# Scans of a state-space layer: B and C spread over the channels by DMA through DRAM, products with B on GpSimd, sums of neighbours by identity products on TensorE

## What is computed

```python
def _ssm_layer(x, A_log, Dp, W_dbc, W_dt, b_dt):
    A = -jnp.exp(A_log)
    dbc = jnp.einsum('ble,ce->blc', x, W_dbc)
    delta, Bm, Cm = jnp.split(dbc, [DT_RANK, DT_RANK + N_STATE], axis=-1)
    delta = jax.nn.softplus(jnp.einsum('blr,er->ble', delta, W_dt) + b_dt)
    dA = jnp.exp(delta[..., None] * A)
    dBx = (delta * x)[..., None] * Bm[:, :, None, :]
    _, hs = jax.lax.associative_scan(combine, (dA, dBx), axis=1)   # h = dA * h_before + dBx
    y = jnp.einsum('blen,bln->ble', hs, Cm)
    return y + Dp * x
for i in range(3):
    x = _ssm_layer(x, ...)
    if i < 2:                                # neighbours in time are averaged: 750, 375, 187 steps
        x = x[:, :l // 2 * 2].reshape(b, l // 2, 2, d).mean(axis=2)
```

## Time and profile before

| | us |
|---|---|
| median of 3 runs | 861.51 (857.21 to 864.0) |
| the profiled execution, its own time | 856.02 |
| its span, first to last instruction | 854.2 |
| first scan starts | 44.5 |
| last unit's last scan starts | 367.4 |
| attention's first matmul | 371.9 |

### The profile page before, as it was taken

How to read it: one execution, slowest core, us unless ns; L and a number is a source line. 1 busy time by engine, 2 the same in 40 slices (tenths; PEclk the granted TensorE clock), 3 DMA queues, 4 the chain that set the end, 5 groups by cost and what they waited for, 6 DMA issues and landing times.

```text
span 854.2 us, 10724 instructions
## 1 busy us (share of the span) xinstructions
PE 749.1 (88%) x3396; PEld 379.1 (44%) x3396; DVE 567.9 (66%) x861; ACT 364.0 (43%) x638; POOL 482.0 (56%) x508
## 2 busy tenths in 40 slices
PE   4689888889888887855998889879999999999997
PEld 2345454545545453423776667733233232323232
DVE  3299899999999996846458888656444444444443
ACT  2345455554545554312454555343333433333332
POOL 2379788888888887423565555343333443334331
PEclk9699999999999998967999999999999999999999
DMA  8200000000000000040000000091933444324400
GB/s 308 66 1 1 1 1 2 0 2 1 2 0 1 1 1 0 1 99 1 1 1 3 5 3 3 10 189 43 204 75 78 91 97 96 84 64 95 102 1 18
DMA packets 19078, 37.40 MB, mean 44 GB/s; under 512 B 2255, under 2 KB 17607, under 8 KB 18375
## 3 DMA queue, kind: packets, MB, share of 16 engines
q1 hardware_dynamic: 18711, 36.01, 18.1%
q10 hardware_dynamic: 304, 0.63, 0.2%
HBM read 34.72 MB, written 1.92 MB: 43 GB/s over the span
## 4 chain that ended last, share of the span: by engine, by line
PE 64%; DVE 16%; ACT 8%; issue 6%; POOL 1%; DVEq 0%; ACTq 0%; POOLq 0%
PE pair L706 21%; PE pair L378 12%; PE pair L714 10%; PE pair L379 5%; PE pair L605 4%; DVE tmp L1089 4%; PE pair L588 3%; PE pair L637 2%; ACT work L757 2%; ACT work L758 2%; DVE pair L1062 1%; PE pair L435 1%; PE pair L467 1%; DVE tmp L1097 1%; ACT pair L764 1%
## 5 line engine op out<-in xcount | busy, mean ns | idle before, releaser
L1337 DVE TENSOR_TENSOR hidden<-pair,tmp 128x502 f32<-128x502 f32 (+1 forms) x192 | 121.7, 675 | 144.3 <-PE pair L706 135.2
L1496 POOL TENSOR_TENSOR hidden<-xs,big 128x502 f32<-128x502 f32 (+1 forms) x96 | 111.4, 1162 | 184.2 <-PE pair L706 165.1
L945 ACT ACTIVATE tmp<-pair 128x502 f32<-128x502 f32 (+1 forms) x192 | 102.5, 587 | 174.6 <-PE pair L706 174.6
L1520 POOL TENSOR_TENSOR big<-big 94x512 f32<-94x512 f32 (+3 forms) x120 | 89.6, 780 | 79.6 <-DVE big L1244 71.0
L706 PE MATMUL pair<-xs,w 64*128 64x502 f32 (+1 forms) x384 | 107.6, 638 | 2.4 <-ACT tmp L945 2.4
L714 PE MATMUL pair<-hidden,w 128*64 128x502 f32 (+1 forms) x384 | 101.9, 609 | 2.5 <-DVE hidden L1337 2.5
L706 PE MATMUL pair<-hidden,w 64*128 64x502 f32 (+1 forms) x384 | 98.0, 586 | 0.4
L1089 DVE TENSOR_TENSOR_SCAN tmp<-tmp,pair 128x750 f32<-128x750 f32 (+1 forms) x56 | 95.5, 1706 | 0.1
L775 ACT ACTIVATE tmp<-big,picked 128x749 f32<-128x749 f32 (+2 forms) x56 | 51.1, 913 | 86.6 <-issue 49.5
L378 PE MATMUL pair<-big,work 128*128 128x512 f32 x128 | 67.5, 609 | 11.9 <-ACT work L758 3.6
L1358 POOL TENSOR_TENSOR big<-big,work 128x750 f32<-128x750 f32 (+1 forms) x28 | 45.5, 1624 | 48.4 <-ACT big L762 48.4
(11 more groups left out here) (187 smaller groups left out, 1262.5 us busy)
## 6 DMA issues: line engine op xcount, KB each, us to landing
big<-dispatched SPq DMA_DIRECT2D x40, 502.0 KB, 6.6
big<-in_x SPq DMA_DIRECT2D x3, 1500.0 KB, 11.2
big<-dispatched SPq DMA_DIRECT2D x8, 498.0 KB, 5.7
w<-in_w SPq DMA_DIRECT2D x5, 512.0 KB, 6.9
big<-in_x SPq DMA_DIRECT2D x4, 375.0 KB, 3.5
out<-resid SPq DMA_DIRECT2D x8, 187.0 KB, 7.3
packed<-in_packed ACTq DMA_DIRECT2D x1, 424.5 KB, 4.5
dispatched<-hidden SPq DMA_DIRECT2D x8, 47.0 KB, 1.5
```

What stands on the lines that cost most here:

```text
L945: act.activation(sT[i % 2][:, 0:w], bank[i % 2][:, 0:w], ACT.Silu).then_inc(silu_a, 1)
L1337: v.tensor_tensor(hidT[i % 4][:, 0:w], bank[2 + i % 2][:, 0:w], sT[i % 2][:, 0:w], ALU.mult)\
L1496: pool.tensor_tensor(xw[e % 4][:, 0:hi - lo], xs[:, lo:hi], wx[:, e, 0:hi - lo], ALU.mult)\
L1520: ins = eng.tensor_tensor(dst[:, :, at:at + H * m].rearrange("p u (h d) -> p u h d", d=m), t[:, :, :, 0:m], t[:, :, :, k:D], ALU.mult)
```

## The change

Per unit, by the diff:

- `weighted_b` and `weighted_c` (four wide products) go. In their place `rows(n)` computes only the eight rows that are wanted (two halves of the batch, B and C, two states) with a 32-column matrix `rowsel`; ACT copies them to SBUF (`rows_out`), SP writes them to a DRAM tensor `rowsd` by two DMAs, waits until they have landed, and reads them back by four DMAs, each of which repeats the rows over 64 partitions: into `Bt` (two) and `Ct` (two), both in SBUF and double-buffered by unit. SP does this in order of units, with its waits in the same queue.
- `load(n, j)`, B times u, moves from DVE to POOL and works in place in `Bt`. `recur` now reads dA and `Bt`, `read` reads h and `Ct`, `corrected` reads W and E: both operands in SBUF.
- `pool_output` and `add` go from POOL. In their place PE adds the three terms and their even and odd halves by products with the identity into one PSUM bank (`sums`: six matmuls of 375 or 374 columns), and ACT copies the sum to the next layer's x (`sums_out`, once per unit, twice in layer 2). h and the skip term get a second buffer each.
- `read(n, 1)` moves to the start of DVE's next period. E gets a second buffer, delta and u a ring of seven units. The steps that choose the states use other PSUM banks and are placed a little differently.
- At the start SP loads x for phases 2 and 3 after the rows of unit 0 and unit 1, and the 15 DMAs of `later` (weights of attention and experts) after those of unit 2.

```diff
-        delta = [big[:, 12000 + 3000 * i:15000 + 3000 * i] for i in range(2)]
-        u = [big[:, 18000 + 3000 * i:21000 + 3000 * i] for i in range(2)]
...
-        dA, hT = two(0, 750), two(1500, 750)
-        PT, y0T, E, R, pT = (work[:, 750 * i:750 * i + 750] for i in range(5))
-        sel = [[[work[:, 3375 + 128 * (4 * i + 2 * j + k):3503 + 128 * (4 * i + 2 * j + k)] for k in range(2)]
-                for j in range(STATIC)] for i in range(2)]
+        dA = two(0, 750)
+        hT = [two(1500, 750), two(5250, 750, work)]
+        PT, R, W = (work[:, 750 * i:750 * i + 750] for i in range(3))
+        E, y0T = two(2250, 750, work), two(3750, 750, work)
+        pT = W
+        rowsel = [sb(f"rowsel{i}", [128, 32]) for i in range(2)]
+        rowsT = [sb(f"rows{i}", [64, 375]) for i in range(2)]
...
+            def spread_rows(n):
+                _, l, w, _ = unit(n)
+                i, half = n % 2, w // 2
+                sp.wait_ge(rw_a, n + 1)
+                after(sp, b_d[i], 32 * (n // 2))
+                after(sp, c_d[i], 32 * (n // 2))
+                for c in range(2):
+                    sp.dma_start(rowsd[i, :, :, :, half * c:half * c + half].rearrange("b k j t -> (b k j) t"),
+                                 rowsT[i][32 * c:32 * c + 8, 0:half]).then_inc(rw_d, 16)
+                sp.wait_ge(rw_d, 32 * (n + 1))
+                for k, (dst, sems) in enumerate(((Bt, b_d), (Ct, c_d))):
+                    after(sp, hc_v if k else sc_v, STATIC * (n - 1))
+                    for b in range(2):
+                        sp.dma_start(dst[i][64 * b:64 * b + 64, :, 0:w],
+                                     rowsd[i, b:b + 1, k, :, 0:w].to_broadcast([64, STATIC, w])).then_inc(sems[i], 16)
             load(0)
             sp.wait_ge(params_in, PARAMS)
...
-            sp.wait_ge(xa_g, STATIC * UNITS)
+            for n in range(UNITS):
+                spread_rows(n)
+                if n == 0:
+                    load(5)
+                elif n == 1:
+                    load(6)
+                elif n == 2:
+                    sp.wait_ge(zeroed, 1)
+                    for dst, src in later:
+                        sp.dma_start(dst, src).then_inc(later_in, 16)
+            sp.wait_ge(xa_a, TAKEN[-1])
...
+            def rows(n):
                 p, _, w, x = unit(n)
                 pe.wait_ge(sel_a, p + 1)
-                if j == 0:
-                    pe.wait_ge(relu_a, min(n + 2, UNITS))
+                after(pe, rw_a, n)
+                for c in range(2):
+                    mm = pe.matmul(bank[4][32 * c:32 * c + 32, 0:w // 2], rowsel[p % 2][:, :],
+                                   x[:, w // 2 * c:w // 2 * c + w // 2], start=True, stop=True)
+                mm.then_inc(rw_p, 1)
...
+            def sums(n, part):
+                _, l, _, _ = unit(n)
+                terms = [y0T[n % 2]] + hT[n % 2]
+                if l < 2:
+                    if part == 0:
+                        after(pe, xa_a, TAKEN[n] - 1)
+                        pe.wait_ge(y_v, n + 1)
+                    pe.wait_ge(hc_v, STATIC * n + part + 1)
+                    for i in ((0, 1), (2,))[part]:
+                        for k, t in enumerate(halves(terms[i], l)):
+                            mm = pe.matmul(parts(bank[5], l), ident, t, start=(i == 0 and k == 0), stop=(i == 2 and k == 1))
+                    if part == 1:
+                        mm.then_inc(pl_p, 1)
                 else:
-                    after(pe, sc_v, STATIC * n)
-                    pe.wait_ge(cor_v, min(n + 2, UNITS))
-                    if n == UB[p] and p:
-                        pe.wait_ge(more_v, MV[p])
-                wide(pairs[j], sel[p % 2][j][0], x, w).then_inc(b_p, 1)
...
+                ends = last_of(n) is not None
+                old = n - 1 if n > 0 and last_of(n - 1) is None else None
+                if n > 0 and last_of(n - 1) is not None:
+                    pe.wait_ge(more_v, MV[last_of(n - 1) + 1])
+                if n > 0 and chain(n - 1)[1] in (0, 1):
+                    pe.wait_ge(dec_v, chain(n - 1)[0] * DECV + (3, 6)[chain(n - 1)[1]])
                 if n + 2 < UNITS:
                     z(n + 2)
-                if here:
-                    weighted_c(n, 1)
+                    if not ahead(n + 2):
+                        rows(n + 2)
+                if old is not None:
+                    sums(old, 0)
                 if q == 0:
...
+                if 0 <= n + 1 < UNITS:
+                    summed(n + 1)
...
+                if old is not None:
+                    sums(old, 1)
...
                 if n + 2 < UNITS:
-                    if q == 0:
-                        pe.wait_ge(dec_v, p * DECV + 2)
                     mixed(n + 2)
-                if last_of(n) is not None:
+                    if ahead(n + 2):
+                        rows(n + 2)
+                if q == 0:
+                    extremes_row(p, 0)
+                    extremes_spread(p, 0)
+                elif q == 1:
+                    ranks_and_quadratic(p, 0)
+                if ends:
+                    sums(n, 0)
+                    sums(n, 1)
                     more_slots(last_of(n))
...
-                act.wait_ge(exp_a, n + 1)
-                act.activation(d, e, ACT.Ln, bias=1.0).then_inc(log_a, 1)
-                after(act, sc_v, STATIC * (n - 1))
-                act.activation(pairs[1][:, 0:w], e, ACT.Identity, bias=1.0).then_inc(one_a, 1)
+                z, d, e = pairs[0][:, 0:w], of(delta, n), E[n % 2][:, 0:w]
+                if part == 0:
+                    act.wait_ge(z_p, n + 1)
+                    after(act, dl_g, n - 1)
+                    act.activation(e, z, ACT.Abs, bias=bdt[:, l:l + 1]).then_inc(abs_a, 1)
+                    after(act, sum_g, n)
+                    act.activation(R[:, 0:w], z, ACT.Relu, bias=bdt[:, l:l + 1]).then_inc(relu_a, 1)
+                else:
+                    act.wait_ge(abs_a, n + 1)
+                    act.activation(e, e, ACT.Exp, scale=-1.0).then_inc(exp_a, 1)
+                    act.wait_ge(exp_a, n + 1)
+                    act.activation(d, e, ACT.Ln, bias=1.0).then_inc(log_a, 1)
...
+            def rows_out(n):
+                _, _, w, _ = unit(n)
+                act.wait_ge(rw_p, n + 1)
+                after(act, rw_d, 32 * (n - 1))
+                act.activation(rowsT[n % 2][:, 0:w // 2], bank[4][0:64, 0:w // 2], ACT.Copy).then_inc(rw_a, 1)
+            def sums_out(n, part):
+                p, l, _, _ = unit(n)
+                act.wait_ge(pl_p, TAKEN[n] - TAKES[n] + part + 1)
+                dst = pooled(n)
+                if l == 2:
+                    dst = dst[:, 2 * part:2 * part + 2, :]
+                act.activation(dst, parts(bank[5], min(l, 1)), ACT.Copy).then_inc(xa_a, 1)
...
+                if n + 2 < UNITS:
+                    softplus(n + 2, 0)
+                    if not ahead(n + 2):
+                        rows_out(n + 2)
+                    softplus(n + 2, 1)
+                if old is not None:
+                    sums_out(old, 0)
                 if 0 <= n + 1 < UNITS:
                     decay(n + 1, 0)
-                if n + 2 < UNITS:
-                    softplus(n + 2)
+                if old is not None and TAKES[old] == 2:
+                    sums_out(old, 1)
...
+                if n + 2 < UNITS and ahead(n + 2):
+                    rows_out(n + 2)
                 if last_of(n) is not None:
+                    for part in range(TAKES[n]):
+                        sums_out(n, part)
...
-            def load(n, j):
-                _, _, w, _ = unit(n)
-                bu = pairs[j][:, 0:w]
-                v.wait_ge(b_p, STATIC * n + j + 1)
-                v.wait_ge(u_g, n + 1)
-                v.tensor_tensor(bu, bu, of(u, n), ALU.mult).then_inc(bu_v, 1)
+                if n > 1:
+                    v.wait_ge(pl_p, TAKEN[n - 2])
+                v.scalar_tensor_tensor(y0T[n % 2][:, 0:w], pairs[1][:, 0:w], dskip[:, l:l + 1], x, ALU.add, ALU.mult)\
+                    .then_inc(y_v, 1)
             def recur(n, j):
                 p, l, w, _ = unit(n)
                 v.wait_ge(dk_a, STATIC * n + j + 1)
-                if n:
-                    after(v, hf_g if PHASES[PH[n - 1]][0] < 2 else xa_g, STATIC * (n - 1) + j + 1)
+                v.wait_ge(bu_g, STATIC * n + j + 1)
+                if n > 1:
+                    v.wait_ge(pl_p, TAKEN[n - 2])
                 if j == 1 and n == UB[p] and p:
                     v.wait_ge(more_g, MG[p])
-                v.wait_ge(bu_v, STATIC * n + j + 1)
-                v.tensor_tensor_scan(hT[j][:, 0:w], dA[j][:, 0:w], pairs[j][:, 0:w], 0.0, ALU.mult, ALU.add)\
+                v.tensor_tensor_scan(hT[n % 2][j][:, 0:w], dA[j][:, 0:w], Bt[n % 2][:, j, 0:w], 0.0, ALU.mult, ALU.add)\
                     .then_inc(sc_v, 1)
...
-                v.wait_ge(c_p, STATIC * n + j + 1)
+                h = hT[n % 2][j][:, 0:w]
```

(31 more changed lines are left out.)

228 lines of the change are left out of this document (94 added, 134 removed).

## The result

The changed kernel takes 941.47 us (median of 4 runs, 939.06 to 943.08) against 859.36 us (4 runs, 857.2 to 864.0): ratio 1.0945, 95% interval 1.0887 to 1.1003. The prediction said 940 us. The profiled execution took 941.99 us with a span of 940.1, 85.9 more than the span before.

A forecast was written before the change was run, and what follows sets the result against it. DVE bounds the kernel before; in the changed one, exclusion between DVE and POOL gives 14.4 us a unit against 11.56: 68 us, plus start 4 and tail 11, 83 more, so 940 us, range 865 to 985.

The forecast's parts named there:

- The step that carried it: Scans: DVE's scans, `read`, `corrected` (6.20 us) and POOL's 8.71 us can't overlap, 14.9 us a unit before savings.
- that rival: Scans: they take no part in the exclusion; about 11.8 us a unit, 874 us in all; chance 0.10.
- Nothing binds: Scans: no exclusion binds and the change does what it is made for; 10.4 us a unit, 837 us; chance 0.08.
- 13.3 + 0.4: Each unit: 14.9 us of excluding work less 1.6 spared at handovers, plus 0.4 for imperfect order.
- the 0.4 for imperfect order: Each unit: DVE and POOL both wait at times where their order is not perfect; 0.4 us added.
- 0.7 a unit: Choice steps on POOL now lie on the path of the scans, adding 0.7 us per unit.
- taken at half that or a little more, 2.9 us a phase: POOL's eight small choice operations, the longest 0.61 us, priced at half that or a little more; 2.9 us a phase.
- Strict alternation of five and five: Each unit: five DVE and five POOL operations take turns, sparing 1.6 us; 13.3 us per unit.
- POOL and DVE each near 14 us busy of 14.4: Sign in the profile after: both engines near 14 us busy per 14.4 us unit, since waiting counts as busy.
- What was costed at nothing: Each unit: DMA (10.3 us, under 13.3), PE and ACT add nothing to the period.
- the clock has its part: PE's granted clock under 0.9 between 100 and 300 us; at half clock 1020 us; clock or DMA chance 0.05.
- Start and tail: Loads at the start add 4 us (0 to 9); unit 24's scan to attention takes 61, 11 more than before.

The follow-up runs named there:

- e3: Kernel before the change, with softplus' last step writing `corrected`'s first operand to SBUF instead of PSUM; 874.54 us, ratio 1.0166.
- e4: Changed kernel with both states' dA in one PSUM pair in turn, `summed` sharing the pair of `mixed`, each state's scan and read together; 943.71 us.
- e8: e4 with `summed` ahead of `sums` on PE, choice steps behind the second scan, scanning in place in PSUM and reading from there; 936.34 us.
- e1: Changed kernel with POOL's `load` multiplying only the first 8 of 750 columns of each unit; 895.67 us.
- e9: e8 with a third skip-term buffer, second half of `sums` behind `mixed`, choice steps between `output` and second scan, sums' copy behind `decay`; 882.24 us.
- e10: Changed kernel with e9's order on DVE and PE and its third skip-term buffer, but dA, h and the scans in SBUF; 951.98 us.
- e6: Changed kernel with `load` on DVE, in place in SBUF, ahead of each scan; 940.18 us.
- e5: Changed kernel with the choice steps ahead of `corrected` on DVE; 948.65 us.
- e2: Changed kernel with the four spreads of a unit moving only 8 of 750 columns; 937.07 us.

## Why the prediction was right, point by point

**The bound.** The step that carried it, a DVE instruction with two SBUF operands and a POOL instruction exclude each other whole, holds: shown by e3 (one operand moved, 0.935 to a median of 1.549), by the scans going back to 1.70 in e4 and 1.72 in e8, and by how all stretched instructions end just behind POOL's. That it paces the changed kernel rests on e1 (2.8 us off POOL, 1.83 off the period) and on the 4.3 us a unit that DVE waits in its instructions; e9 against e10 (70 us) agrees, with the reserve on the clock. It is not the whole of it: e4, e6 and e8 took parts of the exclusion away and gained nothing clear, since another wait came in. The exclusion holds for scans too, which no row of before had shown; that rival (874) is out. "Nothing binds" (837) is out for the change, though e9's third and fourth units go at 10.2, the 9.5 to 10.4 that this rival named.

**Per unit, 14.4 forecast, 14.37 measured; the terms were off and cancelled, which is luck.** The base was 13.3 + 0.4. The third and fourth unit of each phase take 12.5 to 13.2, 12.8 on average. One reason is POOL's price: `load` was taken at 1.806 by its nearest row; unhindered it takes 1.64 (mean of e8), and POOL's five sum to 8.2 instead of 8.71. The other would be that the 0.4 for imperfect order wasn't there; this fits the number, and no run shows it by itself.

The choice steps were to cost 0.7 a unit. The first two units of a phase take 14.7 and 17.3 us on average, which makes 1.6 a unit over the whole. The error is in "taken at half that or a little more, 2.9 us a phase": right in sum (2.94 us in before), but taken as plain work. A small POOL step is itself one side of the exclusion and, where it meets one, waits for a long DVE instruction. Two of them after, and the same in e9 (window 100 to 320):

```profile
L1463 POOL TENSOR_SCALAR amax<-packed,low 128x64 f32<-128x64 f32 x4 | 7.7, 1913 | 0.4
L1461 POOL TENSOR_SCALAR low<-low 128x1 f32<-128x1 f32 x4 | 5.7, 1424 | 0.7 <-POOL low L1458 0.7
```
```profile
L1466 POOL TENSOR_SCALAR amax<-packed,low 128x64 f32<-128x64 f32 x5 | 2.3, 465 | 0.5
L1464 POOL TENSOR_SCALAR low<-low 128x1 f32<-128x1 f32 x5 | 1.9, 379 | 0.9 <-POOL low L1461 0.9
```

Not every one of them waits: of the four of the first row one took its 463 ns and two took 2744; `fast`, `slow` and `wBTf` never changed. All eight sum to 7.04 us a phase instead of 2.94, 1.0 more per unit, about what is missing between 0.7 and 1.6. It isn't the only candidate: the first two units of a phase fell by 2.7 us together when the choice stood ahead of `corrected` (e5), so the chain through PE has a part. So 12.8 and 1.6 stood for 13.7 and 0.7.

**"Strict alternation of five and five" was wrong.** POOL finished its addition and ran two more instructions past a waiting `corrected` (187.76 above), and four past `read` in e5. What this did to the sum, no run separates. What is spared at a handover was right: 0.93 - 0.81 = 0.12 us there, 0.13 forecast.

**"POOL and DVE each near 14 us busy of 14.4"** was half right. DVE has 93% (13.4 us), POOL 82% (11.8): over the scans POOL waited 50.7 us for ACT's logarithm and 24.4 for `corrected`, in gaps that my sum of the two engines' work didn't have.

**What was costed at nothing.** DMA: right (e2; POOL waited 6.4 us for it in all). PE: busy 76 to 81 of 100 us, not 60, in part since its clock was granted at 0.85 to 0.91, where before had 1.00. I had said that under 0.9 the clock has its part. z at 192.78 is an instance, 1 us late by the clock. How much of 14.37 it makes was not separated by any run. The waits through PE that e8 ran into I had not looked for at all: the sum by engines has PE at 8.6, and such a loop isn't work but waits across engines.

**Start and tail.** The four first units cost 13.3 us more than before, 2.8 each by the period and 1.9 beyond it, where 4 (0 to 9) was forecast. The tail came to 61.9 (61): unit 24 to 25 23.0 (24), 25 to 26 13.9 (13.8), the rest 25.0 (23). The rest of the program gave 4.2 us more, unchanged in code and not in the forecast. In sum 85.9 us on the profiled execution where 83 was forecast, with errors of a few us that partly cancel.

## What to carry to other kernels

Before an operand is moved from PSUM to SBUF, look at which instructions then have two SBUF operands, and add their time to all of POOL's, small steps included, since each can cost a wait for a whole instruction of the other engine. The sign is a row whose min is its old value and whose median isn't: this is a wait, though the page counts it as busy and lists no releaser. When a theory's cure shows in the row but not in the time (e4, e8), read what waits now before dropping the theory; here the cure was worth 5 us at most and the new order less than nothing, and both together 59. No order tried made the change faster than the kernel before.

## What was not expected of the hardware

- Who comes next isn't alternating: POOL kept DVE out over three instructions in a row (4.65 us for one of 0.93, up to 5.92), and over four in e5 (7.50).
- Very small POOL instructions can wait as long as big ones: 128x64 took up to 2.744 us (1.913 on average in four) instead of 0.465, 128x1 up to 1.882 (1.424) instead of 0.379.
- The exclusion has no exception for a scan, though a scan takes 2.3 ns per element: its median went from 1.706 to 2.748 us, and back to 1.705 with dA in PSUM.
